# A graph layer kernel: the last supertile's scores ahead of its fourth projection tile, and its attention transpose ahead of the fourth output tile

## Chip, cores and metric

The kernel runs on one core of a Trainium2 chip. The metric is the device time of one execution in microseconds (us), as the median of several runs. TensorE is called PE, VectorE DVE, ScalarE ACT, GpSimd POOL and SyncE SP.

## The reference

128 graphs of 64 nodes with 384 features each. Cut to what matters (the bias terms b1, b2, gcn_b and bo are kept in the kernel; `hi` and `hj` also hold a term of the dependency type):

```
h = maximum(layernorm(x), 0)
hi = h @ W1[:384] + dep @ W1[384:] + b1
hj = h @ W2[:384] + dep @ W2[384:] + b2
relevance = sum(hi * hj, -1)            # 64 x 64 per graph
A = softmax(where(adj != 0, relevance, -1e9), axis=2)
out = x + relu((A @ h) @ gcn_w + gcn_b) @ Wo_w + Wo_b
```

## The kernel before, in words

The 128 graphs are cut into 16 supertiles of 8 graphs: 4 tiles (k) of 128 rows, of 2 graphs (g) each. LAST is 15, KT is 4, GT is 2, DC is 3 (384 = 3 x 128) and S is 64. Float32 values are split into a high and a low float16 part, so each projection is three matmuls per contraction chunk (L1174, L1175, L1176).

For supertile s PE does, in `iteration`: three chunks of g (`g_chunk`, h times the folded W1 and W2, 512 columns); hg tile 0 (`hg_tile` through `free_hg_tile`, h times gcn_w, 385 columns: the last one is a row term for the scores, called row_term here); `aggregation(s)`, which makes z of the supertile before (attention times hg, so z carries gcn_w already); hg tiles 1, 2 and 3; the scores of s (`scored_supertile`, 24 matmuls at L1277 and 24 at L1285, called S below); and `output`, which multiplies z of the supertile before with Wo in four tiles of nine matmuls (called out tiles). Behind the last iteration stand, one after another: the transposes of the last attention (`transposed_attention`, L1390, four of them), the last aggregation (L1423 and L1428) and `last_output` (L1488 to L1494).

The order on each engine is written out by hand, and engines wait for each other by counting semaphores. In the last supertile:

- ACT evicts z (L577 and, in place, L579) and the high part of each hg tile (`hg_high_part`, L584), copies half of the scores to the other 64 partitions (`move_scores`, L646), takes the exponentials (L652), and copies the transposed attention (`attention_out`, L635).
- DVE makes the low part of z (`z_low_part`, L1044), the row term (L929) and the low part of hg (`hg_low_part`, L842); in `masked_scores` it adds the row term to the mask (L1059, four tiles), mask and scores (L1069, once per 64 partitions), the moved half (L1073), and takes the row maximum (L1076) and the bias of the exponential (L1078). `attention` normalises and splits (L1083, L1085, L1094, L1102). `add_output` adds an out tile to x (L1052). `attention_high` copies the transposed attention's high part (L1039).
- SP moves hg's low and high parts to other partitions (`move_hg`, L296 and L297, four transfers of 192 KB per supertile) into the tile hg_parts, which the aggregation reads, and stores the finished supertile (L270; L335 for the last one, tile by tile).
- POOL splits tokens and adds the output bias.

## Time and profile before

| what | value |
|---|---|
| median of 3 runs | 360.76 us (360.28 to 360.89) |
| the profiled execution's own time | 359.88 us |
| its span, first to last instruction | 358.1 us |
| PE busy | 346.7 us (97% of the span) |
| DVE, ACT busy | 264.7 us (74%), 264.9 us (74%) |
| POOL busy | 175.2 us (49%) |

The time of an execution has a little around the span; here 359.88 less 358.1 is 1.8 us. A share of busy time is an average over the span; the last 25 us, in which the last supertile drains, look different from it. All times in the views below count from the start of the span.

### The profile page before, as it was taken

To read this page: it belongs to the slowest core of one execution; us is meant where nothing else is said; L and a number is where in the kernel's file an instruction comes from. 1 tells how busy PE (TensorE), PEld (TensorE's weight loads), DVE (VectorE), ACT (ScalarE), POOL (GpSimd) and SP (SyncE) were. 2 spreads that over 40 slices of the span, in tenths; PEclk is the share of its full clock that TensorE was granted. 3 is DMA by queue.
4 is the path that set the end of the run, shared out by engine and by line. 5 is a ranking of instruction groups with operands and counts; after the bars stand their busy time and mean duration, and the time that the engine had idled before them with its cause. 6 is when DMAs were issued, how large, how long until landed. Compare 5 with 4: busy or idle time off the path is not lost.

```text
span 358.1 us, 9301 instructions
## 1 busy us (share of the span) xinstructions
PE 346.7 (97%) x3068; PEld 213.7 (60%) x3068; DVE 264.7 (74%) x664; ACT 264.9 (74%) x563; POOL 175.2 (49%) x354
## 2 busy tenths in 40 slices
PE   7999999899999999999999999999999999999985
PEld 6766565565657566565656566565756566565753
DVE  0998788686968777785968777695967777586664
ACT  2399896977787977778797877778697877755642
POOL 3067573756637182745638183745628183770000
PEclk9999999999999999999999999999999999999999
DMA  7994608965859395775759395675749383645052
GB/s 230 320 209 141 179 2 176 236 140 120 207 126 231 89 262 119 191 173 121 203 117 249 88 255 125 174 176 128 201 109 266 88 205 90 160 91 154 11 165 100
DMA packets 97000, 57.54 MB, mean 161 GB/s; under 512 B 60450, under 2 KB 96932, under 8 KB 96980
## 3 DMA queue, kind: packets, MB, share of 16 engines
q1 hardware_dynamic: 96272, 56.90, 63.8%
q10 hardware_dynamic: 644, 0.20, 0.3%
q0 software_dynamic: 64, 0.20, 0.2%
q8 instruction: 10, 0.16, 0.2%
q14 instruction: 10, 0.08, 0.1%
HBM read 17.44 MB, written 12.58 MB: 84 GB/s over the span
## 4 chain that ended last, share of the span: by engine, by line
PE 87%; DVE 4%; ACT 4%; DMA 2%; issue 1%; DVEq 0%; SPq 0%; ACTq 0%
PE bank L1174 24%; PE bank L1175 24%; PE bank L1176 24%; PE bank L1428 3%; PE bank L1423 3%; PE bank L1277 3%; PE bank L1285 2%; DMA x_all<-in_L_gnn_W_w_dram 2%; PE bank L1218 2%; ACT bank L652 1%; ACT h_tok L497 1%; PE bank L1488 1%; PE bank L1490 1%; ACT h_parts L497 1%; DVE bank L1069 0%
## 5 line engine op out<-in xcount | busy, mean ns | idle before, releaser
L449 POOL TENSOR_TENSOR h_parts<-h_tok,h_parts 128x1536 f16<-128x1536 f32 (+1 forms) x15 | 43.6, 2907 | 94.4 <-ACT h_parts L497 94.3
L1174 PE MATMUL bank<-gw_hi,hT 128*128 128x385 f16 x192 | 63.1, 328 | 1.6 <-DVE g_parts L924 1.1
L1176 PE MATMUL bank<-gw_hi,hT 128*128 128x385 f16 x192 | 62.7, 327 | 0.0
L425 POOL TENSOR_TENSOR x_all<-x_all,bo_all 128x1536 f32 (+1 forms) x16 | 55.0, 3442 | 15.7 <-ACT h_tok L515 15.7
L1175 PE MATMUL bank<-gw_lo,hT 128*128 128x385 f16 x192 | 62.6, 326 | 0.0
L924 DVE TENSOR_TENSOR g_parts<-bank,g_parts 128x512 f16<-128x512 f32 x48 | 33.2, 691 | 36.0 <-ACT bank L570 35.8
L1174 PE MATMUL bank<-wo_hi,z_hi 128*128 128x384 f16 x180 | 58.9, 327 | 0.5 <-DVE z_lo L1044 0.5
L1176 PE MATMUL bank<-wo_hi,z_lo 128*128 128x384 f16 x180 | 58.7, 326 | 0.0
L1175 PE MATMUL bank<-wo_lo,z_hi 128*128 128x384 f16 x180 | 58.7, 326 | 0.0
L1174 PE MATMUL bank<-hT,m_hi 128*128 128x512 f16 x144 | 54.6, 379 | 0.7 <-DVE hT L747 0.7
L1175 PE MATMUL bank<-hT,m_hi 128*128 128x512 f16 x144 | 54.6, 379 | 0.0
L1176 PE MATMUL bank<-hT,m_lo 128*128 128x512 f16 x144 | 54.6, 379 | 0.0
L565 ACT ACTIVATE g_parts<-bank,pair_bias 128x512 f16<-128x512 f32 x48 | 32.9, 685 | 21.0 <-PE bank L1176 21.0
L577 ACT ACTIVATE z_hi<-bank,gcn_bias 128x512 f16<-128x512 f32 x48 | 33.7, 703 | 12.3 <-PE bank L1428 12.3
L1044 DVE TENSOR_TENSOR z_lo<-bank,z_hi 128x512 f16<-128x512 f32 x48 | 32.9, 685 | 9.0 <-ACT bank L579 8.8
L584 ACT ACTIVATE hg_hi<-bank 128x384 f16<-128x384 f32 x64 | 32.3, 511 | 7.8 <-PE bank L1176 7.7
L1052 DVE SCALAR_TENSOR_TENSOR x_all<-bank,out_scale,x_all 128x384 f32 (+1 forms) x64 | 36.3, 610 | 1.6 <-PE bank L1494 1.5
L497 ACT ACTIVATE h_tok<-x_all,ln_add,ln_mul 128x384 f32 (+1 forms) x52 | 36.5, 703 | 0.3
L497 ACT ACTIVATE h_parts<-x_all,ln_add,ln_mul 128x384 f16 (+1 forms) x52 | 36.4, 699 | 0.0
L842 DVE SCALAR_TENSOR_TENSOR hg_lo<-bank,hg_hi 128x384 f16<-128x384 f32 x64 | 35.1, 548 | 0.0
L579 ACT ACTIVATE bank<-bank,gcn_bias 128x512 f32<-128x512 f32 x48 | 32.6, 679 | 0.0
L570 ACT ACTIVATE bank<-bank,pair_bias 128x512 f32<-128x512 f32 x48 | 31.3, 652 | 0.0
(165 smaller groups left out, 644.2 us busy)
## 6 DMA issues: line engine op xcount, KB each, us to landing
x_all<-in_x_dram SPq DMA_DIRECT2D x16, 768.0 KB, 6.9
out_dram<-x_all SPq DMA_DIRECT2D x15, 768.0 KB, 5.2
hg_parts<-hg_lo SPq DMA_DIRECT2D x32, 192.0 KB, 3.6
hg_parts<-hg_hi SPq DMA_DIRECT2D x32, 192.0 KB, 3.9
x_all<-in_L_gnn_W_w_dram SPq DMA_DIRECT2D x2, 576.0 KB, 5.2
out_dram<-x_all SPq DMA_DIRECT2D x4, 192.0 KB, 1.9
gcn_raw<-in_L_gnn_gcn_w_dram SPq DMA_DIRECT2D x1, 576.0 KB, 10.8
x_all<-in_L_gnn_Wo_w_dram SPq DMA_DIRECT2D x1, 576.0 KB, 11.5
```

The costliest lines, as they stand in the source:

```text
L425: nc.gpsimd.tensor_tensor(x_all[:, s, :, :], x_all[:, s, :, :], bo_all[:, :, :].broadcast_to([P, KT, D]), ALU.add).then_inc(x_biased, 1)
L449: ins = nc.gpsimd.tensor_tensor(h_parts[:, at, 1, :], h_tok[:, at, :], h_parts[:, at, 0, :], ALU.subtract)
L497: nc.scalar.activation(to, x_all[:, s, k, :], ACT.Relu, bias=ln_add[:, k:k + 1], scale=ln_mul[:, k:k + 1]).then_inc(h_ready, 1)
L565: nc.scalar.activation(g_parts[:, c, :, 0, :], g_bank[c], ACT.Identity, bias=pair_bias[:, c:c + 1], scale=PROJ).then_inc(g_high, 1)
L577: nc.scalar.activation(z_hi[:, c, :], z_bank, ACT.Relu, bias=gcn_bias[:, c:c + 1], scale=Z_DOWN).then_inc(z_high, 1)
L842: nc.vector.scalar_tensor_tensor(hg_lo[:, k, :], bank[hg_banks(s)[k]][:, 0:D], PROJ, hg_hi[:, k, :], ALU.mult, ALU.subtract).then_inc(hg_s ...
L924: nc.vector.tensor_tensor(g_parts[:, c, :, 1, :], g_bank[c], g_parts[:, c, :, 0, :], ALU.subtract).then_inc(g_split, 1)
L1044: nc.vector.tensor_tensor(z_lo[:, c, :], z_bank, z_hi[:, c, :], ALU.subtract).then_inc(z_split, 1)
L1052: nc.vector.scalar_tensor_tensor(x_all[:, s, k, :], bank[O_BANK[k]][:, 0:D], out_scale[:, 0:1], x_all[:, s, k, :], ALU.mult, ALU.add).then ...
L1174: nc.tensor.matmul(dst, lh, rh, start=(c == 0), stop=False)
L1175: nc.tensor.matmul(dst, lh, rl, start=False, stop=False)
L1176: last = nc.tensor.matmul(dst, ll, rh, start=False, stop=(c == DC - 1))
```

## The change

It concerns the last supertile alone. The loop over the earlier ones is the same code.

- PE: S stands ahead of hg tile 3 instead of behind it. The four attention transposes stand ahead of the fourth out tile. The last aggregation takes the eight 64-column matmuls of a chunk (which read hg_parts) first and the four 128-column ones (which read hg_hi) last, and waits for `attT_high` only between them.
- DVE: the row term of hg tile 2 is taken straight after that tile's matmuls; three masks with their row term and a plain copy of the fourth mask follow; then z's third low part and the sum of the scores. The row term of tile 3 is made afterwards (`last_row`) and added to the fourth tile of the summed scores. The low parts of hg tiles 2 and 3 come behind the exponential's bias. The additions of the out tiles are spread: tile 0 ahead of `attention`, tile 1 behind it, 2 and 3 behind `attention_high`.
- ACT: the high part of hg tile 2 waits for that tile's row term, and tile 3's comes behind `move_scores`.
- SP: hg_parts is filled in six transfers: two with the low parts of tiles 0 and 1 (96 KB each), two with all high parts, two with the low parts of tiles 2 and 3.

```diff
+    def move_last_hg():
+        def move_part(lanes, part, tiles):
+            for g in range(GT):
+                sp.dma_start(hg_parts[lanes, tiles, g, :], part[g * S:(g + 1) * S, tiles, :])                          .then_inc(hg_moved, 16)
+        sp.wait_ge(z_done, DC * LAST)
+        sp.wait_ge(hg_split, KT * LAST + 2)
+        move_part(slice(0, S), hg_lo, slice(0, 2))
+        sp.wait_ge(hg_high, KT * (LAST + 1))
+        move_part(slice(S, 2 * S), hg_hi, slice(0, KT))
+        sp.wait_ge(hg_split, KT * (LAST + 1))
+        move_part(slice(0, S), hg_lo, slice(2, KT))
...
-        move_hg(s + 1)
         if s + 1 < LAST:
+            move_hg(s + 1)
             transpose_attention(s + 1)
+        else:
+            move_last_hg()
         store_out(s)
...
                 act.wait_ge(z_done, DC * s)
+            if c == 2 and last:
+                act.wait_ge(row_ready, KT * s + DC)
             hg_high_part(s, c)
-        hg_high_part(s, DC)
+        if not last:
+            hg_high_part(s, DC)
...
+        if isinstance(s, int) and s == LAST:
+            act.wait_ge(row_ready, KT * NSUP)
+            hg_high_part(s, DC)
...
     def rows_and_low(s, k):
         dve.wait_ge(hg_high, KT * s + k + 1)
+        row_of(s, k)
+        hg_low_part(s, k)
+    def row_of(s, k):
         nc.vector.tensor_scalar(row_term[:, k:k + 1], bank[hg_banks(s)[k]][:, D:D + 1], Y_SCALE,
                                 pq_scaled[:, 0:1], ALU.mult, ALU.add).then_inc(row_ready, 1)
-        hg_low_part(s, k)
...
+    def last_masks():
+        dve.wait_ge(row_ready, KT * LAST + DC)
+        for k in range(DC):
+            nc.vector.tensor_scalar(masks[:, k, :], bias_all[:, KT * LAST + k, :], row_term[:, k:k + 1],
+                                    None, ALU.add).then_inc(masked, 1)
+        nc.vector.tensor_copy(masks[:, DC, :], bias_all[:, KT * LAST + DC, :]).then_inc(masked, 1)
+    def last_row():
+        dve.wait_ge(hg_done, KT * NSUP)
+        row_of(LAST, DC)
+        dve.wait_ge(row_ready, KT * NSUP)
+        dve.wait_ge(scored, LAST + 1)
+        nc.vector.tensor_scalar(scores[:, DC, :], scores[:, DC, :], row_term[:, DC:DC + 1], None,
+                                ALU.add).then_inc(scored, 1)
+    def masked_scores(s, last=False):
+        if not last:
+            all_masks(s)
...
-        dve.wait_ge(scored, s + 1)
+        if last:
+            last_row()
+        dve.wait_ge(scored, s + 2 if last else s + 1)
...
         for c in range(DC):
+            if c == 2 and isinstance(s, int) and s == LAST:
+                last_aggregated()
+                return
...
+    def last_aggregated():
+        dve.wait_ge(hg_done, KT * LAST + DC)
+        row_of(LAST, 2)
+        last_masks()
+        z_low_part(LAST - 1, 2, bank[Z_BANK[2]][:, :])
+        masked_scores(LAST, last=True)
+        hg_low_part(LAST, 2)
+        hg_low_part(LAST, DC)
+        add_output(LAST - 1, range(1))
+        attention(LAST)
+        add_output(LAST - 1, range(1, 2))
...
     attention_high(2)
+    add_output(LAST - 1, range(2, KT))
...
-            if isinstance(s, int) and s > LAST and c == 2:
-                pe.wait_ge(score_copied, GT * NSUP)
-                pe.wait_ge(summed, GT * NSUP)
...
+    def last_aggregation():
+        pe.wait_ge(attT_copied, 2)
+        hg_read(KT * NSUP)
+        pe.wait_ge(score_copied, GT * NSUP)
+        pe.wait_ge(summed, GT * NSUP)
+        pe.wait_ge(hg_moved, MOVES * LAST + 16 * 3 * GT)
+        for c in range(DC):
+            for k in range(KT):
+                for g in range(GT):
+                    at = k * P + g * S
+                    nc.tensor.matmul(bank[LAST_Z_BANK[c]][:, at:at + S], hg_parts[:, k, g, c * P:(c + 1) * P],
+                                     attT_parts[:, k, g, :], start=(k == 0 and g == 0), stop=False,
+                                     skip_group_check=True)
+            pe.wait_ge(attT_high, GT * 2)
+            for k in range(KT):
+                last = nc.tensor.matmul(bank[LAST_Z_BANK[c]][:, k * P:(k + 1) * P],
+                                        hg_hi[:, k, c * P:(c + 1) * P], attT_hi[:, k, :, :], start=False,
+                                        stop=True, skip_group_check=True)
+            last.then_inc(z_done, 1)
...
+            if k == DC and isinstance(s, int) and s == LAST:
+                transposed_attention(LAST + 1)
...
+        last = isinstance(s, int) and s == LAST
         for k in range(KT):
+            if last and k == DC:
+                scored_supertile(s, half)
             free_hg_tile(s, k, half)
             if k == 0:
                 aggregation(s, Z_BANK)
-        scored_supertile(s, half)
+        if not last:
+            scored_supertile(s, half)
         output(s)
...
-    transposed_attention(LAST + 1)
-    aggregation(LAST + 1, LAST_Z_BANK)
+    last_aggregation()
     last_output()
```

PE before, at the end of hg tile 3 (into bank 0) and the beginning of out (into bank 3); bank 6 holds the scores:

```order
L1175 MATMUL bank0<-gw_lo,hT1 128x385
L1176 MATMUL bank0<-gw_hi,hT1 128x385
L1277 MATMUL bank6<-hT1,g_parts 128x64 [waits summed,score_copied,g_split]
L1277 MATMUL bank6<-hT1,g_parts 128x64 x23
L1285 MATMUL bank6<-hT1,g_parts 64x64 x24
L1174 MATMUL bank3<-wo_hi,z_hi 128x384 [waits z_split]
L1175 MATMUL bank3<-wo_lo,z_hi 128x384
```

PE in the changed kernel: the end of hg tile 2 (bank 2), S, and hg tile 3, with the rows in front of out:

```order
L1243 MATMUL bank2<-gw_lo,hT1 128x385
L1244 MATMUL bank2<-gw_hi,hT1 128x385
L1345 MATMUL bank6<-hT1,g_parts 128x64 [waits summed,score_copied,g_split]
L1345 MATMUL bank6<-hT1,g_parts 128x64 x23
L1353 MATMUL bank6<-hT1,g_parts 64x64 x24
L1242 MATMUL bank0<-gw_hi,hT1 128x385 [waits hg_split]
...
L1243 MATMUL bank0<-gw_lo,hT1 128x385
L1244 MATMUL bank0<-gw_hi,hT1 128x385
L1242 MATMUL bank3<-wo_hi,z_hi 128x384 [waits z_split]
```

S moved ahead of the nine matmuls of hg tile 3; the first out tile still follows both.

PE before, from the last out tile (bank 2) over the transposes (bank 7) to the last aggregation:

```order
L1176 MATMUL bank2<-wo_hi,z_lo 128x384
L1390 MATMUL bank7<-ident16,att_all 128x128 [waits attT_copied,attT_high,att_ready]
L1390 MATMUL bank7<-ident16,att_all 128x128 x3
L1423 MATMUL bank0<-attT_all,hg_hi 128x128 [waits hg_split,hg_moved,attT_copied,attT_high]
L1428 MATMUL bank0<-attT_all,hg_parts 128x64 x2
L1423 MATMUL bank0<-attT_all,hg_hi 128x128
```

PE in the changed kernel, the same place: the third out tile (bank 5), the transposes, the fourth out tile, and the aggregation:

```order
L1244 MATMUL bank5<-wo_hi,z_lo 128x384
L1458 MATMUL bank7<-ident16,att_all 128x128 [waits attT_copied,attT_high,att_ready]
L1458 MATMUL bank7<-ident16,att_all 128x128 x3
L1242 MATMUL bank2<-wo_hi,z_hi 128x384 [waits hg_split]
...
L1244 MATMUL bank2<-wo_hi,z_lo 128x384
L1506 MATMUL bank0<-attT_all,hg_parts 128x64 [waits summed,score_copied,hg_moved,hg_split,attT_copied]
L1506 MATMUL bank0<-attT_all,hg_parts 128x64 x7
L1511 MATMUL bank0<-attT_all,hg_hi 128x128 [waits attT_high]
L1511 MATMUL bank0<-attT_all,hg_hi 128x128 x3
```

The fourth out tile moved behind the transposes, and the aggregation's first wait no longer names attT_high.

DVE before, from the low part of z's third chunk to the reciprocal of the row sums:

```order
L1044 TENSOR_TENSOR z_lo<-bank5,z_hi 128x512 [waits z_copied]
L929 TENSOR_SCALAR row_term<-bank2,pq_scaled 128x1 [waits hg_high]
L842 SCALAR_TENSOR_TENSOR hg_lo<-bank2,hg_hi 128x384 [waits hg_moved,hg_high]
L929 TENSOR_SCALAR row_term<-bank0,pq_scaled 128x1 [waits hg_high]
L842 SCALAR_TENSOR_TENSOR hg_lo<-bank0,hg_hi 128x384 [waits hg_moved,hg_high]
L1059 TENSOR_SCALAR masks<-adj_all,row_term 128x64 [waits row_ready]
L1059 TENSOR_SCALAR masks<-adj_all,row_term 128x64 x3
L1069 TENSOR_TENSOR bank7<-bank6,masks 64x256 [waits masked,s_done]
L1069 TENSOR_TENSOR bank7<-bank6,masks 64x256 [waits score_copied]
L1073 TENSOR_TENSOR bank7<-bank7,score_moved 128x256 [waits score_copied,summed]
L1076 TENSOR_REDUCE row_max<-bank7 128x4 [waits scored]
L1078 TENSOR_SCALAR exp_bias<-row_max,exp_nscale 128x4 [waits maxed]
```

DVE in the changed kernel, from the row term of hg tile 2:

```order
L958 TENSOR_SCALAR row_term<-bank2,pq_scaled 128x1 [waits hg_done]
L1094 TENSOR_SCALAR masks<-adj_all,row_term 128x64 [waits row_ready]
L1094 TENSOR_SCALAR masks<-adj_all,row_term 128x64 x2
L1096 COPY masks<-adj_all 128x64
L1072 TENSOR_TENSOR z_lo<-bank5,z_hi 128x512 [waits z_copied]
L1118 TENSOR_TENSOR bank7<-bank6,masks 64x256 [waits masked,s_done]
L1118 TENSOR_TENSOR bank7<-bank6,masks 64x256 [waits score_copied]
L1122 TENSOR_TENSOR bank7<-bank7,score_moved 128x256 [waits score_copied,summed]
L958 TENSOR_SCALAR row_term<-bank0,pq_scaled 128x1 [waits hg_done]
L1104 TENSOR_SCALAR bank7<-bank7,row_term 128x64 [waits scored,row_ready]
L1127 TENSOR_REDUCE row_max<-bank7 128x4 [waits scored]
L1129 TENSOR_SCALAR exp_bias<-row_max,exp_nscale 128x4 [waits maxed]
```

Behind this stand, in the changed kernel, the low parts of hg tiles 2 and 3 and one out tile's addition, and then the reciprocal. Both low parts left the place ahead of the masks; one row term and a 128x64 addition came between the last sum and the row maximum.

## Rows read from the trace of the kernel before

**Rows 1.** The page: 40 slices of POOL, granted clock; chain shares by engine.

```profile
POOL 3067573756637182745638183745628183770000
PEclk9999999999999999999999999999999999999999
...
PE 87%; DVE 4%; ACT 4%; DMA 2%; issue 1%; DVEq 0%; SPq 0%; ACTq 0%
```

**Rows 2.** Timeline of PE, last supertile: start, us, line, op [idle before <-releaser].

```profile
336.14 0.33 PE L1174 MATMUL bank<-gw_hi,hT 128*128 128x385 f16 x1
...
337.62 0.86 PE L1277 MATMUL bank<-hT,g_parts 128*128 128x64 f16 x24
...
338.91 0.34 PE L1174 MATMUL bank<-wo_hi,z_hi 128*128 128x384 f16 x1
...
343.31 0.33 PE L1174 MATMUL bank<-wo_hi,z_hi 128*128 128x384 f16 x1
...
345.31 0.40 PE L1390 MATMUL bank<-ident,att_all 128*128 128x128 f16 x4 [0.38 <-DVE att_all L1102]
347.04 0.23 PE L1423 MATMUL bank<-attT_all,hg_hi 128*128 128x128 f16 x1 [1.32 <-DVE attT_all L1039]
...
348.44 0.34 PE L1488 MATMUL bank<-wo_hi,z_hi 128*128 128x384 f16 x1
```

**Rows 3.** Timeline of DVE, same stretch.

```profile
336.02 0.55 DVE L842 SCALAR_TENSOR_TENSOR hg_lo<-bank,hg_hi 128x384 f16<-128x384 f32 x1
336.83 0.69 DVE L1044 TENSOR_TENSOR z_lo<-bank,z_hi 128x512 f16<-128x512 f32 x1 [0.26 <-ACT bank L579]
337.43 0.21 DVE L929 TENSOR_SCALAR row_term<-bank,pq_scaled 128x1 f32<-128x1 f32 x1
...
338.94 0.74 DVE L1059 TENSOR_SCALAR masks<-adj_all,row_term 128x64 f32<-128x64 f32 x4
339.78 0.90 DVE L1069 TENSOR_TENSOR bank<-bank,masks 64x256 f32<-64x256 f32 x2
340.72 0.43 DVE L1073 TENSOR_TENSOR bank<-bank,score_moved 128x256 f32<-128x256 f32 x1
341.19 0.42 DVE L1076 TENSOR_REDUCE row_max<-bank 128x4 f32<-128x256 f32 x1
341.65 0.23 DVE L1078 TENSOR_SCALAR exp_bias<-row_max,exp_nscale 128x4 f32<-128x4 f32 x1
341.78 1.14 DVE L1052 SCALAR_TENSOR_TENSOR x_all<-bank,out_scale,x_all 128x384 f32<-128x384 f32 x2
343.69 0.18 DVE L1083 RECIPROCAL row_inv<-row_sum 128x4 f32<-128x4 f32 x1 [0.77 <-ACT bank L652]
...
346.38 0.60 DVE L1039 COPY attT_all<-bank 64x256 f16<-64x256 f16 x2
```

**Rows 4.** Timeline of ACT, same stretch.

```profile
337.82 0.49 ACT L584 ACTIVATE hg_hi<-bank 128x384 f16<-128x384 f32 x1 [0.62 <-PE bank L1176]
339.02 0.38 ACT L646 ACTIVATE score_moved<-bank 64x256 f32<-64x256 f32 x1 [0.71 <-PE bank L1285]
...
345.75 0.60 ACT L635 ACTIVATE attT_all<-bank 128x512 f16<-128x512 f16 x1 [2.09 <-PE bank L1390]
347.70 0.69 ACT L577 ACTIVATE z_hi<-bank,gcn_bias 128x512 f16<-128x512 f32 x1 [1.36 <-PE bank L1428]
```

**Rows 5.** Timeline of SP's DMA issues: the store of supertile 14.

```profile
346.33 0.38 SPq L270 DMA_DIRECT2D out_dram<-x_all  x1
```

**Rows 6.** The page's DMA issues of out: count, KB each, median us to landing.

```profile
out_dram<-x_all SPq DMA_DIRECT2D x15, 768.0 KB, 5.2
```

**Rows 7.** The tile hg_parts, whole run: issue ns, first and last start; landing.

```profile
L296 SPq DMA_DIRECT2D hg_parts<-hg_lo x32: 601/621/708, 36.4 to 340.4; - x32
L297 SPq DMA_DIRECT2D hg_parts<-hg_hi x32: 605/660/1063, 37.1 to 341.1; - x32
...
DMA to landing us min/median/max: 2.8/3.7/5.1
```

More of the change, by code:

```diff
@@ L1054, in add_output, with all_masks @@
                                                    ALU.mult, ALU.add).then_inc(o_added, 1)
-            def masked_scores(s):
+            def all_masks(s):
                 dve.wait_ge(row_ready, KT * (s + 1))
@@ L1402, in aggregation @@
             def aggregation(s, z_bank):
-                if isinstance(s, int) and s in (1, LAST + 1):
-                    made = 1 if s == 1 else 2
-                    pe.wait_ge(attT_high, GT * made)
-                    pe.wait_ge(attT_copied, made)
+                if isinstance(s, int) and s == 1:
+                    pe.wait_ge(attT_high, GT)
+                    pe.wait_ge(attT_copied, 1)
                 else:
@@ L1471, in iteration @@
                     g_chunk(c, half, chunk_ready(s) if c == 0 else None)
+                last = isinstance(s, int) and s == LAST
                 for k in range(KT):
+                    if last and k == DC:
+                        scored_supertile(s, half)
                     free_hg_tile(s, k, half)
```

## Prediction

> **What bounds the kernel now.** First the page: the chain that ended last lies on PE for 87%, and PE's granted clock is full in all 40 slices [rows 1]. The loop is bound by PE, and the change leaves it alone. What can move is the end, where PE runs out of work. So I read PE's timeline from hg tile 3 on [rows 2]: hg tile 3 starts at 336.14, S at 337.62, out at 338.91, its fourth tile at 343.31, and the transposes at 345.31. 27 matmuls of out take 4.40 us (338.91 to 343.31), 0.163 each, so nine take 1.47 and out is through at about 344.77. PE then does nothing until 345.31, the transposes take 0.24, and it does nothing again until 347.04, where the last aggregation starts. From there on it has work: the aggregation takes 1.40 (to 348.44) and the last output follows at once. Idle in front of 347.04 are 0.54 and 1.49 us, together 2.03.
>
> Who is late? DVE's timeline [rows 3] and ACT's [rows 4] show one chain: S ends, ACT starts to copy scores at 339.02, DVE is still making masks (338.94, four in 0.74) and begins the sum only at 339.78, then comes the last sum at 340.72, the maximum at 341.19, the exponential's bias at 341.65, ACT's exponentials, the reciprocal at 343.69, DVE's split, and the transposes at 345.31. ACT copies them at 345.75, DVE copies the high part at 346.38 for 0.60 (to 346.98), and PE starts. So the start of S and what DVE does between S and the maximum set the end, and out hides all but 2.03 us of it.
>
> **The change part by part.** *S ahead of hg tile 3.* S starts at 336.14 instead of 337.62, 1.48 earlier; ACT's copy may start at 339.02 - 1.48 = 337.54. Hg tile 3 and out together start where they did: out at 338.91.
>
> *DVE up to the first sum.* The low part of hg tile 1 starts at 336.02 and lasts 0.55; the next instruction starts about 0.09 before such an end (z's low part, 336.83 + 0.69 = 337.52, is followed at 337.43) [rows 3]. So the row term of tile 2 starts at 336.48, its tile having been finished at about 336.34. It takes 0.21; a DVE instruction that waits for the one ahead starts 0.04 after its end (340.72 + 0.43 to 341.19). Masks from 336.73, for 0.74; z's low part from 337.38, which before could start only at 336.83 and so finds its input ready; the sum 0.60 later (336.83 to 337.43), at 337.98. S has been ready for 0.4 us by then. [...]
>
> *The two new operations.* The last sum comes 0.94 after the first (339.78 to 340.72): 338.92. The row term of tile 3 can start 0.34 later, at 339.26; hg tile 3 ends at 338.91 - 0.16 + 0.33 = 339.08, so it does not wait. 0.21 + 0.04 brings 339.51. The 128x64 addition on the scores has no row of its own. Below it lie the reciprocal's 0.18, above it the maximum's 0.42 for 256 columns; the nearest is a mask of 128x64, 0.25 (in each group of four, 0.74 with three starts 0.16 apart). I take 0.25 + 0.04. The maximum starts at 339.80 instead of 341.19: 1.39 earlier. With 0.18 it is 1.46, with 0.42 it is 1.22.
>
> [...]
>
> *From the maximum to the transposes.* The operations are the same, so they shift as one, if DVE is free for the reciprocal. It now has two low parts of hg and one out addition in that gap: from 339.80 + (341.78 - 341.19) = 340.39, twice 0.46 and once 0.57, to 341.9; the reciprocal is due at 343.69 - 1.39 = 342.30. 0.4 us remain, so they cost nothing; without this gap they would cost their 1.5 us. ACT's high part of hg tile 3 starts at 339.54 and lasts 0.49 [rows 4], ahead of the exponentials at about 340.5. The transposes can start at 345.31 - 1.39 = 343.92.
>
> *The transposes ahead of the fourth out tile.* Three out tiles end at 343.31, so PE waits 0.61 there. The transposes take 0.24, the fourth tile 1.47: 345.63. Meanwhile ACT and DVE copy: 346.98 - 1.39 = 345.59. The fourth tile thus fills the hole in which PE waited for these copies, and the aggregation can start at 345.65. Splitting the wait for `attT_high` off is worth nothing here, since it is over by then.
>
> *The six transfers.* The high parts wait for ACT's fourth one: 340.03, and SP issues at 340.07. An issue takes 0.60 to 1.06, in the median 0.62 and 0.66 [rows 7]. The two end at 341.39. The last two wait for DVE's low part of tile 3: 340.39 + 0.46 + 0.55 = 341.40. Issued at 341.45 and 342.07, they land 2.8 to 5.1 later [rows 7], at 344.9 to 347.2. I take 2.8: they are half as large as those in the row, and the queue in front of them is nearly empty, like in front of the transfer that took 2.8. They have until 345.65, so 0.7 us to spare.
>
> *Behind.* The aggregation has the same matmuls per chunk, 1.40 in all; the ACT eviction follows its first chunk as before (347.04 to 347.70) and the last output, which starts 1.40 after the aggregation, needs it at that distance. The out additions of tiles 2 and 3 run from 345.6 to 346.8, while banks are wanted from 347.05 on. The store of supertile 14 is issued at about 346.85, not 346.33 [rows 5], and lands 5.2 later [rows 6], at 352.05; the last stores come behind 27 matmuls and an addition, at 347.05 + 4.40 + 0.57 = 352.0 at the earliest. They hardly meet.
>
> **The sum.** The aggregation starts at 345.65 instead of 347.04, and all behind it is the same work: 1.39 us. The profiled execution took 359.88, so it would take 358.5. The median of the runs lies 0.88 above the profiled one, at 360.76: 359.4.
>
> **The rivals.**
>
> *The attention is not ready earlier (no change).* PE now stands at the transposes with the fourth out tile behind them, so each 0.1 us that the attention comes later costs 0.1. If the new order on DVE lets the sum wait (for the row term, for z's low part, for ACT, which now waits for DVE twice), the 1.39 shrink; if they go altogether, transposes at 345.31, fourth tile to 347.02, aggregation at 347.04: 360.8. For it: four new waits between DVE, ACT and PE. Against it: each waits for something that the rows put 0.1 to 0.4 us ahead. Half eaten gives 360.1.
>
> *The last low parts land late (slower).* The aggregation waits for all six transfers, of which the last two are issued a microsecond later than the last of before (341.1) [rows 7]. From a landing at 345.65, 3.6 us after the second issue, each further microsecond costs one. At 5.1 the aggregation starts at 347.2: 360.9. If all four issues took the worst 1.06, 1.06, 0.71 and 0.71, the last would start at 342.90 and land at 348.0, 1.0 later than PE's start of before: 361.8. It is slower from a landing 5.0 after the issue. Against it: in this stretch no other transfer runs, and the long landings are those of a full queue.
>
> [...]
>
> *The attention comes earlier than I think (faster still).* PE's 0.61 of waiting at 343.31 is the most that there is to win: 1.39 + 0.61 = 2.0, 358.8. It takes a DVE that does masks, sums and row terms in less than the rows' time.
>
> **How the numbers follow.** A measurement of this kernel tells a difference of about 0.2% (0.7 us) from none. Main case, a gain of 1.1 to 1.7, 359.1 to 359.8: 0.70. Faster still, to 358.8: 0.06. The gain more than half eaten or gone, 360.1 to 361.4: 0.16. Late landing, 360.5 to 361.8: 0.08. The range 358.8 to 360.5 leaves the worse half of the last two outside, less than 2 in 10. Faster by over 0.2% takes in the first two, 0.76; within 0.2% most of the third and half of the fourth, 0.17; slower 0.07.
>
> **What would show it.** In the profile after: S starts near 336.1 and hg tile 3 behind it near 337.4; DVE's first sum near 338.0, the maximum near 339.8; PE idle for 0.6 ahead of the transposes near 343.9, then nothing idle up to the aggregation near 345.65, whose releaser, if any, is not a DMA. I am wrong if PE waits at the aggregation for a transfer, if the wait at the transposes is above 1.3 us, or if the last output waits for z's high part or for an out addition.

## The result, and the profile after

The changed kernel takes 357.99 us in the median of six runs (357.88 to 358.09), the kernel before 360.27 (360.20 to 360.89) in six: a ratio of 0.9932, with a 95% interval of 0.9919 to 0.9944. Measured again on another occasion it was 357.87 against 359.87, 0.9945 [0.9931 to 0.9958]. So it is faster by 2.0 to 2.3 us. The forecast was faster by 1.4, at 359.4 with a range from 358.8: the direction was right, and the time is below the range.

The profiled execution took 357.89 with a span of 356.1, that of before 359.88 with 358.1. Between the two profiles lie 1.99 us, and the part outside the span is 1.8 in both. The page of the changed kernel, its span and the chain's shares, against [rows 1]:

```profile
span 356.1 us, 9307 instructions
...
PE 87%; ACT 4%; DVE 4%; DMA 2%; issue 2%; DVEq 0%; SPq 0%; ACTq 0%
```

Nothing moved between the engines on a large scale. What changed is seen in the last 20 us. PE's timeline of the changed kernel, against [rows 2] (start, duration, line, operation, and in brackets idle time before it and what ended it):

```profile
336.11 0.86 PE L1345 MATMUL bank<-hT,g_parts 128*128 128x64 f16 x24
...
337.40 0.34 PE L1242 MATMUL bank<-gw_hi,hT 128*128 128x385 f16 x1
...
338.89 0.33 PE L1242 MATMUL bank<-wo_hi,z_hi 128*128 128x384 f16 x1
...
343.11 0.33 PE L1244 MATMUL bank<-wo_hi,z_lo 128*128 128x384 f16 x1
343.76 0.40 PE L1458 MATMUL bank<-ident,att_all 128*128 128x128 f16 x4 [0.32 <-DVE att_all L1153]
344.00 0.33 PE L1242 MATMUL bank<-wo_hi,z_hi 128*128 128x384 f16 x1
...
345.30 0.33 PE L1244 MATMUL bank<-wo_hi,z_lo 128*128 128x384 f16 x1
345.46 0.40 PE L1506 MATMUL bank<-attT_all,hg_parts 128*128 128x64 f16 x8
345.69 0.39 PE L1511 MATMUL bank<-attT_all,hg_hi 128*128 128x128 f16 x4
...
346.86 0.34 PE L1578 MATMUL bank<-wo_hi,z_hi 128*128 128x384 f16 x1
...
350.77 2.11 PE L1584 MATMUL bank<-wo_hi,z_lo 128*128 128x384 f16 x12
```

S starts at 336.11, hg tile 3 behind it at 337.40, out at 338.89. The transposes wait for DVE, until 343.76; from there PE has no gap up to the end. The aggregation starts at 345.46 with no releaser. DVE, against [rows 3]:

```profile
336.45 0.21 DVE L958 TENSOR_SCALAR row_term<-bank,pq_scaled 128x1 f32<-128x1 f32 x1
336.69 0.58 DVE L1094 TENSOR_SCALAR masks<-adj_all,row_term 128x64 f32<-128x64 f32 x3
337.19 0.19 DVE L1096 COPY masks<-adj_all 128x64 f32<-128x64 f32 x1
337.29 0.68 DVE L1072 TENSOR_TENSOR z_lo<-bank,z_hi 128x512 f16<-128x512 f32 x1
337.89 0.89 DVE L1118 TENSOR_TENSOR bank<-bank,masks 64x256 f32<-64x256 f32 x2
338.82 0.43 DVE L1122 TENSOR_TENSOR bank<-bank,score_moved 128x256 f32<-128x256 f32 x1
339.16 0.21 DVE L958 TENSOR_SCALAR row_term<-bank,pq_scaled 128x1 f32<-128x1 f32 x1
339.40 0.29 DVE L1104 TENSOR_SCALAR bank<-bank,row_term 128x64 f32<-128x64 f32 x1
339.73 0.42 DVE L1127 TENSOR_REDUCE row_max<-bank 128x4 f32<-128x256 f32 x1
...
340.33 1.01 DVE L867 SCALAR_TENSOR_TENSOR hg_lo<-bank,hg_hi 128x384 f16<-128x384 f32 x2
...
342.14 0.18 DVE L1134 RECIPROCAL row_inv<-row_sum 128x4 f32<-128x4 f32 x1 [0.28 <-ACT bank L668]
...
344.82 0.60 DVE L1067 COPY attT_all<-bank 64x256 f16<-64x256 f16 x2 [0.60 <-ACT attT_all L651]
...
351.53 2.19 DVE L1080 SCALAR_TENSOR_TENSOR x_all<-bank,out_scale,x_all 128x384 f32<-128x384 f32 x4 [1.14 <-PE bank L1584]
```

The row maximum comes at 339.73. The new addition L1104 takes 0.29, and the low parts (L867 x2) and one out addition lie behind the exponential's bias, finished 0.28 before the reciprocal. ACT's copy of the transposed attention, against [rows 4], which the aggregation waits for (the store of [rows 5] is now issued at 346.63):

```profile
344.20 0.60 ACT L651 ACTIVATE attT_all<-bank 128x512 f16<-128x512 f16 x1 [2.09 <-PE bank L1458]
```

SP's:

```profile
339.92 1.25 SPq L303 DMA_DIRECT2D hg_parts<-hg_hi  x2
341.55 1.25 SPq L303 DMA_DIRECT2D hg_parts<-hg_lo  x2
```

And the answer on the tile hg_parts in the last stretch, against [rows 7], the time from issue to landing:

```profile
DMA to landing us min/median/max: 2.7/3.0/3.5
```

The last pair is issued at 341.55 and 342.2; the last transfer had landed at 345.04 by the trace's records, 0.42 before PE wanted it.

So far the aggregation starts 1.58 earlier, but the profiles are 1.99 apart. The rest is at the very end. The last additions of before, the timeline of all engines in the stretch behind [rows 2, 3]:

```profile
352.36 2.11 PE L1494 MATMUL bank<-wo_hi,z_lo 128*128 128x384 f16 x12
353.50 2.19 DVE L1052 SCALAR_TENSOR_TENSOR x_all<-bank,out_scale,x_all 128x384 f32<-128x384 f32 x4 [1.53 <-PE bank L1494]
```

L1494 in before and L1584 in the changed kernel are the last 12 matmuls, three for each tile of 128 rows. Before, DVE's first addition starts 1.14 behind the first of them (352.36 to 353.50), in the changed kernel 0.76 (350.77 to 351.53). The same work with the same wait in front, and 0.38 us less. No term of the forecast has this.

### The profile page after: what moved, and what is told of

It reads as the page before. It is cut to its first block, busy times and chain, and to the rows that moved or that the text cites. A ratio compares the mean times of both kernels' runs of the same rounds, so it can differ in the third digit from the quotient of the medians.

```text
span 356.1 us, 9307 instructions
## 1 busy us (share of the span) xinstructions
PE 346.9 (97%) x3068; PEld 214.0 (60%) x3068; DVE 264.8 (74%) x665; ACT 264.9 (74%) x563; POOL 175.3 (49%) x354
## 4 chain that ended last, share of the span: by engine, by line
PE 87%; ACT 4%; DVE 4%; DMA 2%; issue 2%; DVEq 0%; SPq 0%; ACTq 0%
PE bank L1242 24%; PE bank L1243 24%; PE bank L1244 24%; PE bank L1491 3%; PE bank L1486 3%; PE bank L1345 3%; PE bank L1353 2%; DMA x_all<-in_L_gnn_W_w_dram 2%; PE bank L1286 2%; ACT bank L668 1%; ACT bank L595 1%; ACT h_tok L513 1%; PE bank L1578 1%; PE bank L1580 1%; ACT h_parts L513 1%
## 5 line engine op out<-in xcount | busy, mean ns | idle before, releaser
L867 DVE SCALAR_TENSOR_TENSOR hg_lo<-bank,hg_hi 128x384 f16<-128x384 f32 x64 | 34.9, 547 | 0.0
```

The costliest lines, as they stand in the source:

```text
L867: nc.vector.scalar_tensor_tensor(hg_lo[:, k, :], bank[hg_banks(s)[k]][:, 0:D], PROJ, hg_hi[:, k, :], ALU.mult, ALU.subtract).then_inc(hg_s ...
```

## The experiments

Two sorts of number are used. The profile of each kernel gives distances: from the start of S (or, where S stands behind hg tile 3, of that tile, the point that the code reaches at the same time) to the end of the last addition, called **the tail**. It is free of the scatter of the start, S of the same code coming between 335.95 and 336.11 in two profiles. And the median span of all runs of a kernel is free of what lies outside of the span. The tail of before is 19.55 (336.14 to 355.69), that of the changed kernel 17.61 (336.11 to 353.72): 1.94 less.

| kernel | median us (range, runs) | before beside it | ratio [95%] | median span | tail |
|---|---|---|---|---|---|
| before | medians 359.87 to 360.18 (75 runs in four sets) | | | 358.1 | 19.55 |
| changed | 357.87 (357.74 to 358.17, 5) | 359.87 | 0.9945 [0.9931, 0.9958] | 356.1 | 17.61 |
| s_behind | 359.98 (358.91 to 361.15, 12) | 359.99 | 0.9996 [0.9984, 1.0007] | 357.4 | 18.72 |
| att_behind | 358.91 (358.71 to 359.02, 6) | 359.99 | 0.9971 [0.9959, 0.9982] | 357.1 | 18.37 |
| att_alone | 359.94 (359.63 to 360.08, 11) | 360.18 | 0.9993 [0.9984, 1.0002] | 358.1 | 19.55 |
| four_moves | 359.96 (359.62 to 360.25, 11) | 360.18 | 0.9995 [0.9986, 1.0004] | 358.1 | 19.67 |
| wait_in_front | 358.14 (357.86 to 358.21, 5) | 360.18 | 0.9940 [0.9926, 0.9953] | 356.2 | 17.71 |
| att_inside | 358.17 (357.65 to 358.73, 5) | 360.18 | 0.9940 [0.9926, 0.9953] | 356.1 | 17.57 |
| after_less3 | 358.50 (358.12 to 358.70, 5) | 359.99 | 0.9960 [0.9947, 0.9973] | 356.7 | 18.00 |
| after_pad124 | 357.95 (357.92 to 358.33, 5) | 359.87 | 0.9948 [0.9935, 0.9962] | 356.1 | 17.60 |
| after_pad125 | 358.35 (358.24 to 358.66, 5) | 359.87 | 0.9958 [0.9944, 0.9972] | 356.4 | 18.00 |
| before_pad1 | 359.95 (359.59 to 360.57, 11) | 359.99 | 1.0003 [0.9994, 1.0011] | 357.8 | 19.16 |
| before_pad16 | 359.60 (359.38 to 360.63, 11) | 359.87 | 0.9996 [0.9987, 1.0005] | 357.7 | 19.16 |

**after_again** is the changed kernel as it is, beside others of its set.

> The changed kernel once more, beside the next three on one chip, as their reference. It should stand at a ratio of 0.993 to the kernel before, with the first of the last four additions 0.11 us after its matmul's end, and a profiled time 1.8 us above its span.

It gave 357.87, 2.00 below before, with the first of the last additions 107 ns behind its matmul and 1.8 us outside the span in its profile. Its numbers stand in the row of the changed kernel, with the tail of the first profile (17.60 in its own).

### What each part is worth

**s_behind.** The changed kernel with S behind hg tile 3 again:

```diff
                 for k in range(KT):
-                    if last and k == DC:
-                        scored_supertile(s, half)
                     free_hg_tile(s, k, half)
...
-                if not last:
-                    scored_supertile(s, half)
+                scored_supertile(s, half)
                 output(s)
```

> The changed kernel with S put back behind hg tile 3 on PE; everything else as changed. My chain of steps: hg tile 3 ends near 337.6 and S near 339.0, so DVE's first sum starts at 339.0 instead of 337.9 and the row maximum at 340.85 instead of 339.73, 1.1 later; the transposes come at 344.9, the fourth out tile ends at 346.6, and the last aggregation starts there, 1.1 us later than in the changed kernel: 359.1. Rival (the gain came from the transposes' place alone): the time stays within 0.3 of 357.99.

Its timeline of all engines, one row of DVE and two of PE:

```profile
339.20 0.90 DVE L1118 TENSOR_TENSOR bank<-bank,masks 64x256 f32<-64x256 f32 x2 [1.01 <-PE bank L1353]
...
345.08 0.40 PE L1458 MATMUL bank<-ident,att_all 128*128 128x128 f16 x4 [1.43 <-DVE att_all L1153]
...
346.78 0.40 PE L1506 MATMUL bank<-attT_all,hg_parts 128*128 128x64 f16 x8
```

DVE's masks and z's low part are done long before, and the first sum waits 1.01 for S. The transposes and the aggregation come 1.11 later than in the changed kernel, counted from the same point: not the 1.48 by which S moved, since in the changed kernel DVE, not S, is what the first sum waits for. The tail says 1.11, the spans 1.3. The median alone would say 2.1, as 8 of these 12 runs have more than 2.0 us outside the span (up to 3.6). So S accounts for 1.11 of the gain, given all the rest of the change.

**att_behind.** The changed kernel with the transposes behind the fourth out tile:

```diff
-                    if k == DC and isinstance(s, int) and s == LAST:
-                        transposed_attention(LAST + 1)
...
             iteration(LAST, 1)
+            transposed_attention(LAST + 1)
             last_aggregation()
```

> The changed kernel with the attention transposes put back behind the fourth out tile on PE; everything else as changed. My chain of steps: out ends at 344.75, the transposes follow at once, ACT and DVE need 1.7 us to copy, and the aggregation starts at 346.5, 1.0 us later than in the changed kernel: 359.0, with PE idle for 1.5 us ahead of it. Since chunk 0 needs the high copies only after its first eight matmuls, it may start 0.3 earlier: 358.7. Rival (S alone brings the gain): within 0.3 of 357.99.

Its timeline of PE:

```profile
344.92 0.39 PE L1458 MATMUL bank<-ident,att_all 128*128 128x128 f16 x4
345.99 0.41 PE L1506 MATMUL bank<-attT_all,hg_parts 128*128 128x64 f16 x8 [0.69 <-ACT attT_all L651]
346.62 0.40 PE L1511 MATMUL bank<-attT_all,hg_hi 128*128 128x128 f16 x4 [0.22 <-DVE attT_all L1067]
```

The transposes start at once at 344.92, since the attention has long been ready, and then PE waits for the copies: 0.69 for ACT's, and 0.22 for DVE's ahead of the 128-column matmuls. The tail is 0.76 longer, near the 0.7 that the expectation has for the split wait. Here the split wait for `attT_high` does something: the first eight matmuls run under DVE's copy.

**att_alone.** The kernel before, with nothing but the transposes ahead of the fourth out tile (and the last two out additions behind `attention_high`, for DVE else would wait for a tile that PE makes only after the attention):

```diff
                 attention(s)
-                add_output(s - 1, range(2, KT))
+                if not (isinstance(s, int) and s == LAST):
+                    add_output(s - 1, range(2, KT))
...
             attention_high(2)
+            add_output(LAST - 1, range(2, KT))
...
+                    if k == DC and isinstance(s, int) and s == LAST:
+                        transposed_attention(LAST + 1)
...
             iteration(LAST, 1)
-            transposed_attention(LAST + 1)
             aggregation(LAST + 1, LAST_Z_BANK)
```

> The kernel before with the transposes ahead of the fourth out tile and nothing else (the additions of out tiles 2 and 3 come behind the high copies, since tile 3 is later than they are). The attention is ready as before, so PE waits for it from 343.3 to 345.3, does the fourth tile until 347.0, and the aggregation starts at 347.0: no change, 0.998 to 1.001. This is the first rival of the prediction, with no part of the attention's gain. DVE's code is as long as before up to the last additions, so the first of these should come 0.5 us behind its matmul as in the kernel before, unless one wait more shifts it away (then 0.4 us faster).

Its timeline of PE, the transposes and the first matmul of the aggregation:

```profile
345.06 0.40 PE L1392 MATMUL bank<-ident,att_all 128*128 128x128 f16 x4 [1.83 <-DVE att_all L1102]
...
346.78 0.23 PE L1425 MATMUL bank<-attT_all,hg_hi 128*128 128x128 f16 x1
```

Nothing is gained: the tail is 19.55 again, the span 358.1. PE stands idle for 1.83 at the transposes and for nothing at the aggregation. The fourth tile hid the wait for the attention before, and the wait for the copies now. The place of the transposes pays only once the attention comes early.

att_alone and s_behind together show one part more. Both have S behind hg tile 3 and the transposes ahead of the fourth out tile; s_behind has the new order on DVE, ACT, SP and in the last aggregation besides. Without the 0.39 at the very end, which att_alone has and s_behind lacks (next section), the tails are 19.16 and 18.72. So the new order, with S in its old place, is worth 0.44, and 0 + 0.44 + 1.11 is the 1.55 that the chain gained. What S would bring with the old order on DVE was not run.

**four_moves.** The changed kernel with the four transfers of before, behind all low parts, while these still stand behind the exponential's bias:

```diff
                 else:
-                    move_last_hg()
+                    move_hg(s + 1)
...
-                pe.wait_ge(hg_moved, MOVES * LAST + 16 * 3 * GT)
+                pe.wait_ge(hg_moved, MOVES * NSUP)
```

> The changed kernel with hg_parts filled in the four transfers of before, all of them behind the low part of hg tile 3. That part ends at 341.8, and before the four took from 339.06 to about 345.1 to land, so they would land at 347.8, 2.4 us behind the aggregation's start: time 2.0 to 2.6 us above the changed kernel, all of the gain lost. Rival (DMA had slack enough): within 0.5 us.

Its timeline of all engines, SP's first and last issue and PE's aggregation:

```profile
341.58 0.60 SPq L296 DMA_DIRECT2D hg_parts<-hg_lo  x1
...
343.55 0.95 SPq L297 DMA_DIRECT2D hg_parts<-hg_hi  x1
...
347.74 0.39 PE L1506 MATMUL bank<-attT_all,hg_parts 128*128 128x64 f16 x8 [1.91 <-DMA hg_parts<-hg_hi]
```

The last issue is at 343.55, the wait at the aggregation is 1.91, named as a DMA, and the tail is 2.06 longer. So with these low parts late, the whole gain hangs on the six transfers. Theirs is no gain of their own (in before, with all low parts early, the last of the four landed at 345.08, in time for 347.04), it is what allows the low parts to stand where they do.

**wait_in_front.** The changed kernel waiting for `attT_high` ahead of the whole last aggregation:

```diff
                 pe.wait_ge(hg_moved, MOVES * LAST + 16 * 3 * GT)
+                pe.wait_ge(attT_high, GT * 2)
                 for c in range(DC):
...
-                    pe.wait_ge(attT_high, GT * 2)
```

> The changed kernel with PE's wait for attT_high put in front of the whole last aggregation, as in the kernel before. In the changed kernel the high copies end at 345.42 and PE starts the aggregation at 345.46, so the wait has nothing to wait for: 0.0 to 0.1 us. Rival (the split wait carries part of the gain): 0.2 us or more slower. Where the transposes stood behind the fourth tile the split did matter (there PE began chunk 0 0.6 us ahead of its high matmuls).

Its timeline of PE, the fourth out tile's last matmul and the aggregation's first ones:

```profile
345.50 0.33 PE L1244 MATMUL bank<-wo_hi,z_lo 128*128 128x384 f16 x1
345.78 0.39 PE L1507 MATMUL bank<-attT_all,hg_parts 128*128 128x64 f16 x8
```

Here the aggregation starts 0.28 after the fourth tile's last matmul, not 0.16, and the tail is 0.10 longer. Small, at the edge of what can be told. It fits the trace: in the changed kernel PE begins to load the aggregation's first weights at 345.30, 0.12 before the copy's end at 345.42, and here that load stands behind the wait.

**att_inside.** The transposes inside the fourth out tile, behind its first three matmuls, and the 64-column matmuls of chunk c + 1 ahead of the 128-column ones of chunk c. It fills the hole ahead of the transposes, to see whether the idle time there can be had:

```diff
+                low_products(0)
                 for c in range(DC):
+                    if c + 1 < DC:
+                        low_products(c + 1)
                     pe.wait_ge(attT_high, GT * 2)
...
                                   lambda e: (wo_hi[:, e, :], wo_lo[:, e, :]),
+                                  (lambda e: transposed_attention(LAST + 1) if e == 1 else None) if inside
+                                  else None).then_inc(o_done, 1)
```

> A version that should beat both: the transposes stand inside the fourth out tile, behind its first three matmuls, which fills PE's 0.49 us of waiting at 343.3, and the last aggregation takes the eight low matmuls of chunk 0 and of chunk 1 ahead of chunk 0's high ones. The fourth tile ends 0.49 earlier, at 344.97; the last transfer lands at 345.04, so the aggregation starts near 345.07; the high copies still end at 345.42, so chunk 0 is done 0.2 us earlier than now and ACT's z, and the last output behind it, come 0.15 to 0.2 us earlier. Rival: the wait for the last transfer or for ACT's copy takes it all, 0.0.

Its timeline of PE:

```profile
343.67 0.40 PE L1458 MATMUL bank<-ident,att_all 128*128 128x128 f16 x4
...
345.09 0.63 PE L1506 MATMUL bank<-attT_all,hg_parts 128*128 128x64 f16 x16
345.55 0.39 PE L1516 MATMUL bank<-attT_all,hg_hi 128*128 128x128 f16 x4
...
346.72 0.34 PE L1584 MATMUL bank<-wo_hi,z_hi 128*128 128x384 f16 x1
```

DVE's copies and ACT's eviction of chunk 0, from the timelines of these engines:

```profile
344.73 0.60 DVE L1067 COPY attT_all<-bank 64x256 f16<-64x256 f16 x2 [0.60 <-ACT attT_all L651]
...
345.98 0.69 ACT L593 ACTIVATE z_hi<-bank,gcn_bias 128x512 f16<-128x512 f32 x1 [1.28 <-PE bank L1516]
```

The hole is gone. Counted from the start of S (336.01 here, 336.11 in the changed kernel), the aggregation starts 9.08 behind it instead of 9.35, at 345.09, right after the last transfer has landed (344.95). But the 128-column matmuls come 9.54 behind S in place of 9.58, and the tail is 0.04 shorter. They do not wait for DVE's copies, which end at 345.33: sixteen 64-column matmuls stand in front of them instead of eight, and these take 0.46 from 345.09. ACT evicts chunk 0 only behind them, at 345.98, and the last output waits for that until 346.72. A second set of five runs gave 358.13 (357.88 to 359.15; before 360.06), with the tail 17.57 again. 

> The version with the transposes inside the fourth tile, once more. In its first profile the last output started 0.13 us earlier than in the changed kernel and the span was as short as the shortest, but the time outside it was 2.8 us and the runs scattered from 357.65 to 358.73. If that is the kernel's own (layout), it repeats: median 358.1 to 358.3, scatter 1 us. If it was chance, the median is 357.7 to 357.8.

Both sets have the span of the changed kernel (356.1 and 356.2), and no version measured here beats the changed kernel clear of the noise. But the limit in this one is partly PE's own order: by the same rows, with eight 64-column matmuls in front, the 128-column ones could follow the copies at about 345.37, an estimate of 0.2 us earlier. That was not run.

### The 0.4 us in front of the last additions

In the trace's own records (ns; DVE's semaphore instruction is the wait for the first tile) the end looks like this:

| kernel | first tile's last matmul ends | wait on DVE starts, lasts | addition starts | late by |
|---|---|---|---|---|
| before | 363514 | 363555, 21 | 364010 | 496 |
| changed | 361857 | 361898, 21 | 361964 | 107 |

DVE takes its wait 41 ns after the matmul in both and is through in 21. Then it stands for another 434 ns before, and for 45 in the changed kernel. So it isn't the semaphore, and no data is missing. My theory was the supply of instructions: between this wait and this addition stands, in before, the edge of a block of DVE's code, and in the changed kernel, whose DVE program is longer by a few instructions, it stands elsewhere. That is a guess; no view of the trace marks such an edge. The rival: the delay belongs to the work (the matmuls' order, banks, semaphores). The page of before lists 10 reads of the kind instruction on queue q14, with 0.08 MB in all; each of them has 8192 bytes. In before, the last starts at 364667, 657 ns behind the late addition.

**before_pad1** and **before_pad16**: before with 1 or 16 more instructions at the start of DVE's program, each a clear of one column of a tile that nobody reads:

```diff
+        pad = sb("pad", [P, 1])
...
         def _(dve):
+            for n in range(1):
+                nc.vector.memset(pad[:, n:n + 1], 0.0)
```

> The kernel before with one more DVE instruction (a clear of one column of an unused tile) ahead of everything; nothing else moves. Theory A (instruction supply): in the kernel before, DVE passed its wait for the first out tile of the last supertile at once (21 ns, in time), but its addition started 0.43 us later, because the instruction behind the wait is the first of a new block of code that had not been read yet. One instruction more shifts the block's edge in front of the wait, where DVE is idle anyway: the first of the last four additions starts about 0.1 us after its matmul instead of 0.5, and the time falls by 0.4 us (up to 0.8, if runs without a profile lose more there), ratio 0.998 to 0.9989. Theory B (the late addition has another cause, in PE or in the tail's data): the addition stays 0.5 us late and the ratio is 1.000.

> The kernel before with 16 more DVE instructions at its start. One more took the late addition away (0.50 to 0.11 us behind its matmul, the span 0.4 shorter apart from the start), but the time did not fall: outside the span it took 2.3 us instead of 1.8, with one more read of code after the end. If that second part hangs on the layout of DVE's code, 16 instructions place it differently: addition 0.11 behind, 1.8 outside, and a ratio of 0.9985 to 0.9992. If the part outside the span is unrelated to DVE's layout, it scatters as before and the ratio is 0.9985 to 1.001 with a wide spread of the runs.

**after_less3**: the changed kernel without three waits on DVE that others imply (two for `x_biased` in `add_output`, one for `z_done` in `attention_high`).

> The changed kernel with three waits less on DVE, all of them implied by others (two for x_biased, one for z_done), which shifts the code behind them by three instructions. Theory A (instruction supply): the edge of the block falls again right behind the wait for the last supertile's first out tile, as it did in the kernel before; the first of the last four additions starts 0.5 us after its matmul's end instead of 0.1, and the time rises from 357.99 to about 358.4 (0.3 to 0.8 more), though three waits are gone. Theory B: no change or up to 0.1 us faster, the addition 0.1 us after its matmul.

**after_pad124** and **after_pad125**: the changed kernel with 124 and 125 such clears. 125 is 128 less the 3 taken away above; that the delay would come back at a distance of 128 was a guess, which no run had shown by then.

> The changed kernel with 124 clears of one column each ahead of DVE's program, which shifts its code by 124 instructions. [...] The addition stays 0.1 us behind its matmul; the clears lie in DVE's idle first 8 us, so the time is that of the changed kernel, up to 0.5 more if they delay the first weights' copies.

> [...] Theory A (instruction supply): the first of the last four additions is 0.5 us behind its matmul again, and the time is 0.4 us above that with 124 clears, from one more instruction of 0.06 us at the start. Theory B (the three waits taken away in the earlier run caused it in another way): no difference between 124 and 125.

The last matmuls and the additions behind them, in the timeline of before_pad1:

```profile
352.19 2.11 PE L1498 MATMUL bank<-wo_hi,z_lo 128*128 128x384 f16 x12
352.94 2.19 DVE L1056 SCALAR_TENSOR_TENSOR x_all<-bank,out_scale,x_all 128x384 f32<-128x384 f32 x4 [1.13 <-PE bank L1498]
```

The same in that of after_pad124:

```profile
350.70 2.11 PE L1588 MATMUL bank<-wo_hi,z_lo 128*128 128x384 f16 x12
351.46 2.19 DVE L1084 SCALAR_TENSOR_TENSOR x_all<-bank,out_scale,x_all 128x384 f32<-128x384 f32 x4 [1.14 <-PE bank L1588]
```

And in that of after_pad125:

```profile
350.75 2.11 PE L1588 MATMUL bank<-wo_hi,z_lo 128*128 128x384 f16 x12
351.89 2.19 DVE L1084 SCALAR_TENSOR_TENSOR x_all<-bank,out_scale,x_all 128x384 f32<-128x384 f32 x4 [1.52 <-PE bank L1588]
```

From the matmuls to the addition it is 0.75 in before_pad1, 0.76 with 124 and 1.14 with 125. By the records the addition is late by 107 with 1 and with 16 clears on before, and by 495 with three waits fewer and with 125 clears on the changed kernel (where the last read on q14 starts 649 ns behind the late addition); by 107 with 124. One instruction turns it on, one turns it off, and a shift of 128 brings it back. The tails follow: 19.16 for 19.55 in before, 18.00 for 17.60 in the changed kernel. The spans too: 357.8 and 357.7 for 358.1. So the delay goes with the place of DVE's code, and the rival falls. In the median of the runs before_pad1 gains nothing, as 8 of its 11 runs have more than 2.0 us outside the span (up to 2.8); before_pad16, with 3 of 11, is 0.27 below before.

The last read on q14 follows the one instruction too: it starts 649 ns behind the start of the first addition with 125 and 1244 with 124, about one addition (534) later. But neither the theory's edge nor that code "had not been read yet" is shown. In before, the last read on q14 ahead of the late addition starts at 344.02 and takes 0.49, which is 9 us too early, and the next one starts behind the addition; no read of code on that queue is under way in the 434 ns. What DVE does in them stays open.

### What lies outside the span

In before_warm18, after_warm18 and inside_warm18 the warm-up at the start has 18 matmuls in place of 10, so that PE's code is longer, to see whether what lies outside the span depends on where code lies.

> The kernel before with eight more warm-up matmuls on PE at the start, where it waits for weights: PE's code is 16 instructions longer, DVE's unchanged. If the part outside the span hangs on PE's layout, profiled time less span and the scatter of the runs change against the kernel before; if not, both stay (1.8, scatter 0.7 to 1.4) or vary by chance. DVE's first last addition stays 0.50 us behind its matmul, since DVE's code did not move. Ratio 0.998 to 1.002.

> The same for the changed kernel. Its time outside the span was 1.8 in each of its profiles and its runs scatter by 0.2 to 0.4 us. If PE's layout matters, 16 instructions may bring the longer outside part: a ratio of 0.995 to 0.997 and a scatter of 1 us. If not, 0.9945 and a scatter of 0.4.

> The same version with PE's code 16 instructions longer at the start. If the part outside the span is a matter of PE's layout, the shift takes it away: outside 1.8, scatter under 0.5, median 357.7, 0.15 below the changed kernel. If it is not, the result is that of the run without the shift.

The pages of before and before_warm18 list 3068 and 3084 matmuls and as many weight loads, so PE executes 32 instructions more, not the 16 of the expectations. The three took 360.50 (359.92 to 361.22, 11 runs; before 360.06), 358.62 (358.53 to 359.26, 5) and 358.25 (358.12 to 359.13, 5). The part outside was 1.8 to 1.9 in all 11, in all 5, and 1.8 to 2.0. The spans grew by 0.6, 0.7 and 0.1 with the longer start; the tails (19.55, 17.62 and 17.56) did not. So no cause is found here: the usual part is 1.8, in every kernel, and some runs have more, before in 16 of 75 more than 2.0 (none of 24 in one set, 11 of 21 in another, up to 3.0), the changed kernel in none of 11. The three profiled executions with more than 2.0 (before_pad1, s_behind, att_inside) each have one more read of code on queue q8 behind the last addition, and the others none. That is a companion and may be a symptom. Why it comes stays open.

## Why the prediction was wrong

Two steps of the prediction's sum failed, the last two: that everything behind the aggregation's start takes as long as before, and that the median lies 0.88 above the profiled execution. The chain up to the aggregation came out within 0.16 us of the 1.39 foreseen. Term by term:

- **What bounds, and what is late: right.** The attention was late, and S and DVE's work up to the row maximum set the end. s_behind and att_alone both show it: without S in front, 1.11 of the gain goes, and the transposes' place alone gives nothing.
- **DVE up to the row maximum: right.** Foreseen were 336.48, 337.98, 339.80 for the row term, the first sum and the maximum; they came at 336.45, 337.89 and 339.73. The new addition took 0.29 for the 0.25 taken from the masks, and masks and z's low part a little less than in their rows. Gain at the maximum, counted from the same point: (341.19 - 336.14) - (339.73 - 336.11) = 1.43, for a forecast of 1.39.
- **Maximum to transposes: nearly the same work.** 4.12 before, 4.03 now, 0.09 less, all of it in ACT's four exponentials up to the reciprocal (1.78 to 1.69 from the first start). Why they are quicker was not tried. From the transposes to the aggregation 1.73 and 1.70. The chain gives 1.43 + 0.09 + 0.03 = 1.55.
- **Transposes ahead of the fourth tile: right.** PE's gap was 0.49 (343.11 + 0.16 to 343.76) for 0.61 foreseen, the fourth tile covered the copies, and att_behind puts a price of 0.76 on the place.
- **"Splitting the wait for `attT_high` off is worth nothing here": nearly.** wait_in_front costs 0.10, as DVE's copy ends at about 345.42, and PE wants its first weights at 345.30.
- **The six transfers: right.** The last one landed at 345.04 for 344.9 foreseen; the six took 2.7 to 3.5 from issue to landing, the four of 96 KB 2.7 to 3.3. The feared late landing did not come.
- **"Behind it is the same work: 1.39 us": wrong.** It is the same work, but it took 0.39 less: DVE's first of the last additions was late by 107 ns in place of 496, and that goes with the place of its code, which the program's new length shifted. That is no merit of the change: after_pad125 has all its edits and lacks the 0.4. The profile of before had the sign: 1.14 us between L1494 and the first of its additions, where three matmuls need 0.65 (two starts of 0.16 and the last one's 0.33). The forecast took its gap as work.
- **"The median of the runs lies 0.88 above the profiled one, at 360.76: 359.4": wrong, and the larger part of the miss.** 0.88 was added to the profiled execution's forecast of 358.5 as if it belonged to the kernel. The changed kernel's median lies 0.10 above its profiled execution. The three runs had gone up to 360.89, while no span of 75 runs of before is above 358.4, and their median is 358.1, as in the profile. So runs at 360.76 and 360.89 must have about 2.4 and 2.5 us or more outside the span, if their spans are like those, and that doesn't carry over. The spans of those three runs themselves are not on record.
- **The lower end of the range, "1.39 + 0.61 = 2.0, 358.8": too high by the same 0.88.** Taken from 359.88, a gain of 2.0 is 357.9. That the profiles are 1.99 apart is a coincidence: 0.49 of the wait at the transposes is still there, and the 0.39 at the end, which no term has, made up for it.

The sum of the miss in the median, 359.4 - 357.99 = 1.4: 0.8 from the surplus of the runs, 0.4 from the place of DVE's code, 0.16 from the chain, the rest rounding and the start. Of the 1.94 in the tails, 1.55 are the change's doing and 0.39 come by chance of the code's place.

## What to carry to other kernels

Forecast the span, and treat the runs' surplus over it as unexplained: never carry it from three runs to another kernel. When a wait is satisfied and the engine still doesn't start for some 0.4 us, ask whether the place of its code matters; adding a single harmless instruction tells (here one clear took before's lateness from 496 to 107 ns), and a gain that one more instruction can give or take isn't credited to an edit. And a part that gives nothing alone, like the transposes here, can be worth most of a microsecond once another part has moved the wait.

## What the runs showed of the hardware

- Right behind a satisfied wait, DVE's first of the last additions started 0.39 us later with its code in some places than in others (496 and 107 ns after the data was there): by the records 495 or 496 in the profiles of before, att_alone, before_warm18, after_less3 and after_pad125, and 106 to 108 in the 13 others. One clear in front of DVE's program took it away in before (496 to 107, before_pad1), one more brought it to the changed kernel (107 to 495, after_pad124 and after_pad125), and after_less3 and after_pad125, which are 128 instructions apart, both have it (495). In none of the five was a read of code under way in the delay, so what the 0.39 us are stays open.
- The time outside of the span is 1.8 us in most executions and up to 3.6 in others, and how often it is more differs between kernels that are the same but for a few instructions (8 of 12 in s_behind, 0 of 6 in att_behind). No cause was found.
